# Turning the score maxima on VectorE instead of TensorE and ScalarE, in a fused attention and mixture-of-experts kernel

## What is computed

```python
c_kv = x @ W_DKV + b_DKV;  c_q = x @ W_DQ + b_DQ
k_c, v_c, q_c = c_kv @ W_UK + b_UK, c_kv @ W_UV + b_UV, c_q @ W_UQ + b_UQ
k_r, q_r = (x @ W_KR + b_KR) * pe, (x @ W_QR + b_QR) * pe
k = concat([split_heads(k_c), repeat(k_r)]);  q = concat([split_heads(q_c), repeat(q_r)])
scores = einsum('bhsd,bhtd->bhst', q, k) / sqrt(32)        # 16 heads, 512 x 512 each
attn = softmax(scores, axis=-1)
x = x + layernorm(einsum('bhst,bhtd->bhsd', attn, v_c) @ W_O + b_O)
```

## Time and profile before

| | |
|---|---|
| three executions | 1570.36, 1573.19, 1573.49 us (median 1573.19) |
| profiled execution, its own time | 1560.94 us |
| its span, first to last instruction | 1559.1 us, mean granted TensorE clock 0.991 |
| busy share of the span | PE 96%, PEld 65%, DVE 63%, ACT 51%, POOL 52% |
| attention | about 40 to 877 us, a unit 23 to 30 us, four units 103 us |

### The profile page before, as it was taken

The page is one execution under the profiler, slowest core; times in us unless marked ns, Lnnn a source line. Parts: engine busy times, 40 slices in busy tenths (PEclk is TensorE's granted clock), DMA queues, the critical chain, the costliest instruction groups (busy, mean ns, idle before and its releaser), DMA issues.

```text
span 1559.1 us, 21757 instructions
## 1 busy us (share of the span) xinstructions
PE 1494.1 (96%) x7006; PEld 1018.1 (65%) x7006; DVE 978.7 (63%) x1846; ACT 795.9 (51%) x1428; POOL 812.2 (52%) x820
## 2 busy tenths in 40 slices
PE   4899999999999999999999999999999999989998
PEld 2555656756656566566654578777666666668886
DVE  5667767676767676767667446862333333359998
ACT  4655567566575665665647355432222222275554
POOL 4358697777786977778769530003222222143341
PEclk9899999999999999999999999999999999999999
DMA  5749489587595895966954431627977777696773
GB/s 156 102 60 175 59 141 208 75 180 140 97 205 81 145 198 73 185 134 104 237 80 114 135 118 41 226 83 230 313 226 207 221 220 216 203 351 221 232 234 132
DMA packets 162758, 255.53 MB, mean 164 GB/s; under 512 B 20052, under 2 KB 70356, under 8 KB 160596
## 3 DMA queue, kind: packets, MB, share of 16 engines
q1 hardware_dynamic: 143336, 202.62, 57.1%
q0 software_dynamic: 12864, 41.96, 9.4%
q10 hardware_dynamic: 6448, 9.57, 1.8%
HBM read 103.87 MB, written 58.46 MB: 104 GB/s over the span
## 4 chain that ended last, share of the span: by engine, by line
PE 72%; DMA 10%; DVE 7%; POOL 4%; ACT 3%; issue 3%; SPq 1%; DVEq 0%; POOLq 0%; ACTq 0%
PE bank L113 12%; PE bank L761 10%; PE bank L829 8%; PE bank L852 8%; PE bank L783 6%; PE bank L666 6%; PE bank L680 6%; PE bank L699 5%; DMA a<-a 5%; PE bank L688 5%; POOL a L1737 2%; PE bank L708 2%; DMA f<-f 2%; PE bank L841 1%; DMA f<-h_scratch,f 1%
## 5 line engine op out<-in xcount | busy, mean ns | idle before, releaser
L1737 POOL TENSOR_TENSOR a<-a 128x512 f32<-128x512 f32 x384 | 500.3, 1331 | 113.0 <-ACT a L1526 66.8
L1526 ACT ACTIVATE a<-bank 128x512 f32<-128x512 f32 x512 | 296.6, 597 | 254.4 <-PE bank L688 213.4
L981 DVE TENSOR_REDUCE a<-bank 128x1 f32<-128x512 f32 x512 | 321.6, 681 | 76.4 <-PE bank L666 76.0
L113 PE MATMUL bank<-a 128*128 128x512 f32 (+1 forms) x864 | 239.0, 398 | 7.0 <-DVE a L957 4.4
L680 PE MATMUL bank<-a 128*128 128x512 f32 x512 | 217.4, 425 | 4.5 <-ACT a L1526 4.4
L688 PE MATMUL bank<-a 68*128 68x512 f32 x512 | 204.0, 398 | 3.8 <-ACT a L1516 3.7
L113 PEld LDWEIGHTS bank<-a 128*128 128x128 f32 (+1 forms) x864 | 159.4, 187 | 53.2 <-issue 8.6
L1801 POOL DMA_INDIRECT f<-h_scratch,f x79 | 76.1, 964 | 225.3 <-DMA f<-f 204.1
L666 PE MATMUL bank<-a 128*128 128x512 f32 x512 | 178.6, 414 | 10.8 <-DVE a L981 5.1
L783 PE MATMUL bank<-c 128*128 128x512 f32 x768 | 179.8, 393 | 4.6 <-ACT c L1582 2.5
L761 PE MATMUL bank<-c 128*128 128x512 f32 x768 | 177.3, 390 | 1.7 <-ACT c L1567 1.6
(11 more groups left out here) (202 smaller groups left out, 1788.5 us busy)
## 6 DMA issues: line engine op xcount, KB each, us to landing
a<-a SPq DMA_DIRECT2D x262, 256.0 KB, 9.6
f<-f SPq DMA_DIRECT2D x316, 64.0 KB
yp_scratch<-f SPq DMA_DIRECT2D x79, 256.0 KB, 3.5
a<-in_L_attn_x SPq DMA_DIRECT2D x15, 1024.0 KB, 7.7
x_scratch<-a SPq DMA_DIRECT2D x8, 1024.0 KB, 4.5
h_scratch<-a SPq DMA_DIRECT2D x8, 1024.0 KB, 13.3
hT_scratch<-s SPq DMA_DIRECT2D x8, 1024.0 KB, 9.9
c<-hT_scratch SPq DMA_DIRECT2D x8, 1024.0 KB, 7.2
```

The costliest lines, as they stand in the source:

```text
L113: t = e.matmul(out, a[n], b[n], start=n == 0 and m == 0, stop=n == len(ah) - 1 and m == 2)
L981: e.tensor_reduce(K.mx[:, i, j:j + 1], K.MX[n % 3][:], AX.X, ALU.max).then_inc(Z.max, 1)
L1526: e.activation(K.pt[:, n % NP, :], K.SC[n % 2][:], ACT.Exp, scale=SCALE).then_inc(Z.exp, 1)
L1737: e.tensor_tensor(K.acc[:, j, :], a, K.pt[:, n % NP, :], ALU.add).then_inc(Z.acc, 1)
```

## The change

`rows` leaves TensorE and ScalarE and becomes a VectorE step. `mx` grows from 4 to 32 columns a tile (the other 28 are set to zero once by GpSimd), VectorE transposes it in 32 x 32 blocks into `mt` (128 x 128), so that partition 32 q + j holds head j of the queries 32 q to 32 q + 31 of each tile, and four `tensor_reduce` with max over an axis of length one and `negate` copy the four partitions of each q into rows 64 to 67 of `QR`. `rows` is no longer among `FILLS`, so that the steps that remain take the two banks in another rhythm. The order list is the same. The rest renames semaphores (`sel` is merged into `set`).

```diff
-FILLS = ("turn", "proj", "half", "rows", "v", "total", "project", "turn2", "route", "fold", "bias")
+FILLS = ("turn", "proj", "half", "v", "total", "project", "turn2", "route", "fold", "bias")
...
-    K.mx = tile([P, 4, 4])
+    K.mx = tile([P, 4, HD])
+    K.mt = tile([P, 4, HD])
...
-    def rows(u):
-        bank = begin("rows", u)
-        w.wait_ge(Z.max, 16 * (u + 1))
-        for i in range(4):
-            t = e.transpose(bank[0:4, i * P:(i + 1) * P], K.mx[:, i, :], K.ident[:])
-        t.then_inc(*end("rows", u))
...
         e.matmul(SC[n % 2][:], K.Kc[z][:, j, i * P:(i + 1) * P], K.Qc[z][:, j, :], start=True, stop=False)
-        drained("rows", u)
+        w.wait_ge(Z.rows, 2 * u + 2)
...
     def top(u, j, i):
         n = 16 * u + 4 * j + i
         w.wait_ge(Z.top, n + 1)
+        w.wait_ge(Z.set, 3)
         if u:
-            m = K.fill["rows", u - 1]
-            w.wait_ge(Z.full[m % 2], m // 2 + 1)
+            w.wait_ge(Z.rows, 2 * u - 1)
         e.tensor_reduce(K.mx[:, i, j:j + 1], K.MX[n % 3][:], AX.X, ALU.max).then_inc(Z.max, 1)
+
+    def rows(u):
+        w.wait_ge(Z.max, 16 * (u + 1))
+        if u >= 2:
+            w.wait_ge(Z.score, 16 * (u - 1))
+        if u:
+            w.wait_ge(Z.rows, 2 * u)
+        e.transpose(K.mt.rearrange("p i r -> p (i r)"), K.mx.rearrange("p i r -> p (i r)")).then_inc(Z.rows, 1)
+        w.wait_ge(Z.rows, 2 * u + 1)
+        tiles = K.QR[64:68, u % 2, :].rearrange("p (i q r) -> p i q r", q=4, r=HD)
+        for q in range(4):
+            t = e.tensor_reduce(tiles[:, :, q, :], K.mt[HD * q:HD * q + 4, :, :].unsqueeze(3), AX.X, ALU.max, negate=True)
+        t.then_inc(Z.rows, 1)
 
     def invert(u):
...
-    def rows(u):
-        b = u // NG
-        bank = begin("rows", u)
-        if u >= 2:
-            w.wait_ge(Z.score, 16 * (u - 1))
-        e.mul(K.QR[64:68, u % 2, :], bank[0:4, :], -1.0).then_inc(*end("rows", u))
...
     e.memset(K.mhalf, -0.5).then_inc(Z.set, 1)
+    e.memset(K.mx, 0.0).then_inc(Z.set, 1)
```

More of the change, by code:

```diff
@@ L384, in __init__ @@
         self.full, self.free = many("ms_full", 2), many("ms_free", 2)
-        self.set, self.small, self.sel, self.rope = make("set_done"), make("dve_step"), make("sel_set"), make("rope_done")
+        self.set, self.small, self.rope = make("pool_set"), make("dve_step"), make("rope_done")
         self.var = {k: make(f"var_{k}") for k in KINDS}
@@ L392, in __init__ @@
         self.x1, self.hi = make("x1_done"), make("kq_high")
-        self.top, self.max = make("top_full"), make("max_done")
+        self.top, self.max, self.rows = make("top_full"), make("max_done"), make("max_rows_step")
         self.score, self.exp, self.acc, self.pv = make("score_full"), make("exp_done"), make("acc_done"), make("pv_done")
@@ L661, in top @@
             w.wait_ge(Z.apart_lo, 2 + 4 + j + 1)
-            w.wait_ge(Z.sel, j + 1)
+            w.wait_ge(Z.set, 4 + j)
         if u == 1:
@@ L686, in scores @@
         w.wait_ge(Z.QR[u % 2], 2 * 16 * (b + 1))
-        w.wait_ge(Z.sel, 6)
+        w.wait_ge(Z.set, 9)
         e.matmul(SC[n % 2][:], K.KR[0:68, b % 2, j, i * P:(i + 1) * P], K.QR[0:68, u % 2, :],
@@ L792, in totals @@
         e.matmul(K.TR[0][:], K.tri, flat, start=True, stop=True).then_inc(Z.totals, 1)
-        w.wait_ge(Z.set, 3)
+        w.wait_ge(Z.set, 10)
         e.matmul(K.TR[1][:], K.onesf, flat, start=True, stop=True).then_inc(Z.totals, 1)
@@ L854, in e_down @@
         t.then_inc(Z.ed, 1)
-    stages = {"turn": turn, "proj": proj, "v": v, "half": half, "plant": plant, "bias": bias, "top": top, "rows": rows, "scores": scores,
+    stages = {"turn": turn, "proj": proj, "v": v, "half": half, "plant": plant, "bias": bias, "top": top, "scores": scores,
               "values": values, "total": total, "project": project, "turn2": turn2, "route": route, "fold": fold, "up": up,
@@ L1398, in finish @@
         e.tensor_tensor(K.x1[:, z, :], K.x1[:, z, :], K.sh[:, z, :], ALU.add).then_inc(Z.co, 1)
-    stages = {"stat": stat, "aggr": aggr, "split w": split_w, "plant low": plant_low, "turn": turn, "low": low, "proj": proj, "half": half, "bias": bias, "top": top, "invert": invert,
+    stages = {"stat": stat, "aggr": aggr, "split w": split_w, "plant low": plant_low, "turn": turn, "low": low, "proj": proj, "half": half, "bias": bias, "top": top, "rows": rows, "invert": invert,
               "project": project, "fold": fold, "split h": split_h, "split up": split_up, "split down": split_down, "up": up,
@@ L1489, in half @@
             w.wait_ge(Z.apart_lo, 2 + 8)
-            w.wait_ge(Z.sel, 4)
+            w.wait_ge(Z.set, 7)
         e.activation(K.kqs[u][:, 2 * n, :], bank[:], ACT.Identity, bias=bias_[:, g:g + 1]).then_inc(Z.hi, 1)
@@ L1684, in finish @@
                      scale=K.crw[:, z, 4, 0:1]).then_inc(Z.cn, 1)
-    stages = {"split w": split_w, "round": round_, "scale": scale, "turn": turn, "proj": proj, "v": v, "half": half, "plant": plant, "repeat": repeat, "rows": rows, "scores": scores, "keep": keep,
+    stages = {"split w": split_w, "round": round_, "scale": scale, "turn": turn, "proj": proj, "v": v, "half": half, "plant": plant, "repeat": repeat, "scores": scores, "keep": keep,
               "turn2": turn2, "route": route, "split h": split_h, "split up": split_up, "round up": round_up,
@@ L1716, in plant @@
             if j:
-                w.wait_ge(Z.sel, j)
-            e.tensor_copy(K.Qc[0][2 * HD:3 * HD, j, :], K.kq[HD * j:HD * (j + 1), 2, :]).then_inc(Z.sel, 1)
+                w.wait_ge(Z.set, 3 + j)
+            e.tensor_copy(K.Qc[0][2 * HD:3 * HD, j, :], K.kq[HD * j:HD * (j + 1), 2, :]).then_inc(Z.set, 1)
         w.wait_ge(Z.w2, 7 * 16)
         for z in range(2):
-            w.wait_ge(Z.sel, 4 + z)
-            e.tensor_copy(K.KR[64:68, z, :, :], K.picks).then_inc(Z.sel, 1)
+            w.wait_ge(Z.set, 7 + z)
+            e.tensor_copy(K.KR[64:68, z, :, :], K.picks).then_inc(Z.set, 1)
     def scores(u, i, j):
```

## The result

The changed kernel takes 1573.59 us (median of 16 executions, 1570.60 to 1578.51) and the kernel before 1570.55 (16 executions, 1566.03 to 1573.53). The medians are 3.0 us apart; the ratio over all executions is 1.0028, with a 95% interval of 1.0017 to 1.0038, which makes it slower by 4.4 us. I had forecast 1.5 us of gain. The absolute time lies in the range, but the sign is wrong.

The account below looks back on a forecast made before the run. TensorE, 96% busy, was taken as the bound, so instructions leaving it pay where it waits for nothing next. Terms -5.0 + 3.0 - 2.0 + 2.5 = -1.5 us, from 1573.19 to 1571.7 us; range 1564 to 1578.

Parts of the forecast that it names:

- The step's own cost: VectorE's transpose, four copies without overlap and two short waits, once per unit: 1.55 us, or 1.2 with overlap.
- kind 2: Step of units 6 to 26, six turns: VectorE delays the next unit's maxima, fifth L666 0.5 later; 3.0 us lost.
- The start: Units 0 to 3: unit 0's opening matmul no longer waits for ScalarE's copy; 2.0 us gained, between 1.45 and 2.6.
- Kinds 0 and 1: First two kinds of turn in a batch of four units, 14 turns: TensorE gains 0.36 each, 5.0 us.
- Kind 1: Second kind, seven turns: TensorE gains 0.36 each; VectorE has 4.39 us idle behind the step.
- Kind 0: First kind, seven turns: TensorE goes on 0.36 earlier; VectorE's 4.13 us of idle time covers the step.
- Kind 3: Units 7 to 27: gain and loss vanish in the next unit's wait for a transfer; nothing.
- Unit 31: Last unit: step behind other VectorE work, 4.9 us late, partly hidden by GpSimd; 2.5 lost, bounds 1.0 and 4.9.
- a rival: Copies slower than expected, each 0.1 us adding 0.4 a turn, in full at kind 2; up to 1592 us; chance 0.19.
- the forecast case: Whole kernel: effect small and of either sign, 1567.8 to 1578.2 us; chance 0.50.
- The worst case of the forecast: Whole kernel, terms at their worst (3.6, 1.45, 4.9) and kind 1 gains halved: +5.0 us.
- slower: Whole kernel slower than before by over 0.2%, 3.1 us; chance 0.21.

Follow-up runs that it names:

- e6: Changed kernel, but all four reduces read partitions 0 to 3; ratio 1.0018 to the kernel before.
- e1: Changed kernel with only unit 31's step moved right behind the last maximum of its unit; ratio 1.0011 to the kernel before.
- e8: Changed kernel with 20 more matmuls in TensorE's idle time ahead of the wait of unit 31; ratio 1.0018 to the kernel before.
- e11: The changed kernel again, unaltered, on another chip; ratio 1.0016 to the kernel before.
- e3: Changed kernel with the step of every unit right behind the unit's last maximum; ratio 0.9954 to the kernel before, 0.9933 on a second chip.
- e2: Changed kernel with the steps of units 2, 6, ..., 30 moved right behind the last maximum of their unit; ratio 0.9991 to the kernel before.
- e9: Changed kernel with one negated reduce over length one, from the first four partitions, in place of the four reduces; ratio 0.9988 to the kernel before.
- e7: Changed kernel with only the steps of units 3 to 27 of kind 3 moved right behind the last maximum; ratio 1.0032 to the kernel before.
- e4: Changed kernel with one plain copy from the first four partitions in place of the four reduces; ratio 1.0245 to the kernel before.

## Why the prediction was wrong, step by step

**The step's own cost** was right. 1.52 us from L983 to the next instruction where I had 1.55, and e6 shows the hold between partition groups that I had taken from the earlier trace rows. (The sum at kind 2 has a slip of 0.1: 414.06 + 1.55 + 2.46 + 0.45 is 418.52, not 418.4.)

**The start** was nearly right: 2.0 us forecast, and 0.4 for the turn of unit 4, against 1.4 measured at unit 0 and 1.8 at unit 4. It varies between executions: where the code is the changed kernel's up to there, unit 4 opens at 151.5 to 153.8 us (after, e1, e8, e11), and before at 154.3 in the one profile that there is. So neither the 2.0 nor the 1.8 is known to better than a microsecond.

**Kinds 0 and 1** were right, a little low in size. Kind 1: unit 8 to 9 takes 28.02 us instead of 28.56, and the six such stretches are 2.9 shorter, 0.47 each. Kind 0: from the first score behind the opening of unit 11 to the opening of unit 12 it takes 23.29 instead of 23.75 us, and 3.0 less over the six, 0.50 each. I had 0.36, the distance in the earlier trace rows. In e3 unit 11 to 12 as a whole takes what it took before (25.29 and 25.32 us), because unit 11 opens earlier there and the first score behind it then waits 0.76 us for a transfer.

**Kind 2 failed, in size.** "the second then ends at 418.4 + 0.60 + 0.68 = 419.7, and the fifth L666 starts 0.5 later than now": 0.5 a turn, 3.0 in all. The mechanism is the one seen, fourth and fifth score wait for the first and second maximum, and for unit 14 even the size is: 0.49. What failed is the step before it, "a batch of four units repeats itself to a tenth of a microsecond, so four turns, one of each kind, stand for 26 of the 32", and with it "the first L666 of unit 15 at 416.98 waits for its transfer". The stretch behind the opening takes 22.25 to 22.31 us at five of the turns before and 22.82 at unit 14, the one that the earlier trace rows show: only there does a wait for a transfer hide part of VectorE's delay. At the other five the step costs 1.03 to 1.07, and the six cost 5.8 us instead of 3.0. e2 takes the six turns out and gains 4.9; e6 and e9 show the cost following the step's length.

**Kind 3** was right: nothing over the four turns up to unit 20 (e7); of the 0.9 us that e7 gains up to unit 28, 0.6 lie at units 22 to 24.

**Unit 31 failed, in size.** I had 2.5, with 4.9 as the bound if nothing hides; it cost 5.3. The queue's part is what I had worked out (2.5 in e8). What is missing is a sentence that I had written and given no price of its own: "An idle stretch of five microseconds may lower TensorE's granted clock for a while." At most the 0.5 between the 2.0 of GpSimd and the 2.5 that I took can stand for it; it cost 2.8 us. The last part of the prediction named it as what would make it wrong; it should have stood in the sum, or at least in the bound, which was no bound without it.

Over units 4 to 28 the sum had -1.3 us (12 x 0.36 gained, 3.0 lost) and it is +1.4; at unit 31 it had +2.5 and it is +5.3. These are 5.5 of the 6 us between forecast and result (-1.5 and +4.4 or +4.6). At unit 31 it is the clock. Over units 4 to 28 it is 2.8 at kind 2 and 1.2 at unit 22, where VectorE and GpSimd meet and of which the prediction has nothing, less 1.5 that kinds 0 and 1 gave more; a few tenths are left. What I called a rival, that each 0.1 us in the step is paid in full at kind 2, was a fact of the forecast case as well. The worst case of the forecast was summed wrongly besides: 3.6 lost at kind 2 and 4.9 at unit 31, 1.45 gained at unit 0 and 3.8 at kinds 0 and 1, with half of kind 1's gain, make +3.3 us, not +5.0, so the measured 4.4 was outside of what its own terms allowed.

The chances gave "slower" 0.21. It is slower by 0.28%, just beyond the bound, and e11 alone (0.16%) would have counted as no change. That the absolute time fell into the range is no merit: the range is 14 us wide.

## What to carry to other kernels

A step that moves to another engine brings its place in a hand-written list with it, and that place was chosen for the old engine. Here the list put the step where TensorE would not wait for the maxima, late; on VectorE the best place is right behind them (1.0028 in the old place, 0.9954 and 0.9933 in the new one, and 1.0313 for the old code in the new place). So price the move at the old place and at the earliest one.

Before one turn stands for six, compare its stretch with the other five. Here 22.82 us against 22.25 to 22.31 would have told that a wait at the shown turn hid half of the cost. And an idle stretch on TensorE is to be priced twice, once for its length and once for the clock behind it.

## What the runs showed of the hardware

After 5.1 us without work TensorE's granted clock was 0.50 and 0.58 in the next two stretches of 3.5 us. With 20 matmuls without use in the idle time it was 1.00 in both, which won 2.8 us.

A VectorE copy with both ends in SBUF can be held behind a whole run of GpSimd's additions (6.43 us instead of 0.42; in e4 five of 32 behind five instructions, 19 behind one). A VectorE instruction with two inputs in SBUF took 1.59 us instead of 0.69 when it began 0.26 us behind a GpSimd addition, and 0.69 when it began 0.03 us ahead of one. A reduce over an axis of length one, which moves the same elements as the copy, was never held (0.677 to 0.679 us in 32 of 32).

Four short reduces start 0.20 us apart when they read one partition group, and 0.29 when they read four.
